# Attention with a gated projection on one core: two key blocks' value products in one run, ten slots for probabilities, four for x

## The reference

```
xn = layernorm(x)
q, k, v = xn @ Wq.T + bq, xn @ Wk.T + bk, xn @ Wv.T + bv        # 16 heads of 32
scores = q @ k.T / sqrt(32)
im = arange(1024) % 256
scores = where(im[:, None] >= im[None, :], scores, -1e30)
s = (softmax(scores) @ v) @ Wo.T + bo
w = (weights >= 0) * 2 - 1
g = silu(clip(xn @ w.T * scale + bias, -100, 100))
out = x + s * g
```

## Time and profile before

| | |
|---|---|
| median of 3 runs | 1834.33 us (1833.07 to 1834.93) |
| the profiled execution | 1834.76 us, of which the span from first to last instruction is 1832.9 us |
| mean granted PE clock | 0.994 |
| PE busy | 1761.5 us (96%), 12184 products |
| DVE busy | 1350.4 us (74%) |
| ACT busy | 977.1 us (53%) |
| POOL busy | 1225.6 us (67%) |

### The profile page before, as it was taken

The page is one execution under the profiler, slowest core; times in us unless marked ns, Lnnn a source line. Parts: engine busy times, 40 slices in busy tenths (PEclk is TensorE's granted clock), DMA queues, the critical chain, the costliest instruction groups (busy, mean ns, idle before and its releaser), DMA issues.

```text
span 1832.9 us, 34064 instructions
## 1 busy us (share of the span) xinstructions
PE 1761.5 (96%) x12184; PEld 796.1 (43%) x12184; DVE 1350.4 (74%) x2518; ACT 977.1 (53%) x1769; POOL 1225.6 (67%) x1066
## 2 busy tenths in 40 slices
PE   5989999999999999999999999999999999999888
PEld 3434444444444444444444444444444444444333
DVE  5878678776777877778777777778678786678652
ACT  4355665465545655456554565555655465554453
POOL 0066657775777567875587855786757775777782
PEclk9999999999999999999999999999999999999999
DMA  6311212221122211222122211222212221122111
GB/s 194 118 26 52 59 36 65 70 70 45 50 60 63 82 42 37 72 59 78 42 53 59 79 55 38 70 58 72 58 38 63 76 53 24 48 63 60 42 47 47
DMA packets 102137, 110.85 MB, mean 60 GB/s; under 512 B 24016, under 2 KB 76368, under 8 KB 101520
## 3 DMA queue, kind: packets, MB, share of 16 engines
q1 hardware_dynamic: 101008, 107.89, 21.4%
q10 hardware_dynamic: 960, 0.79, 0.2%
HBM read 41.23 MB, written 16.78 MB: 32 GB/s over the span
## 4 chain that ended last, share of the span: by engine, by line
PE 85%; DVE 5%; issue 3%; POOL 2%; ACT 2%; SPq 1%; DMA 1%; ACTq 0%; DVEq 0%; POOLq 0%
PE pJ L421 31%; PE pO L613 15%; PE pS L569 10%; PE pT L593 10%; PE pJ L502 3%; PE pT L553 3%; PE pJ L503 3%; PE pJ L506 3%; PE pS L572 3%; PE pT L589 3%; POOL acc L965 2%; DVE mx L873 1%; PE pS L433 1%; ACT PT L725 1%; SPq L1051 1%
## 5 line engine op out<-in xcount | busy, mean ns | idle before, releaser
L965 POOL TENSOR_TENSOR acc<-acc,PT 128x384 f32<-128x384 f32 (+1 forms) x744 | 871.1, 1197 | 402.2 <-PE pO L613 348.1
L873 DVE TENSOR_REDUCE mx<-pS 128x1 f32<-128x512 f32 (+3 forms) x1216 | 776.5, 652 | 273.1 <-PE pS L572 183.7
L725 ACT ACTIVATE PT<-pT 128x512 f32<-128x512 f32 (+1 forms) x960 | 538.1, 567 | 604.1 <-PE pT L593 536.8
L569 PE MATMUL pS<-QK 96*128 96x512 f16 (+3 forms) x1280 | 393.9, 318 | 20.9 <-DVE mx L873 18.1
L593 PE MATMUL pT<-QK 97*128 97x512 f16 (+3 forms) x1280 | 391.6, 317 | 2.6 <-ACT PT L725 1.3
L613 PE MATMUL pO<-PT,V 128*32 128x512 f32 (+3 forms) x2560 | 259.8, 478 | 8.4 <-ACT PT L725 8.2
L569 PEld LDWEIGHTS pS<-QK 96*128 96x128 f16 x1280 | 123.3, 97 | 246.1 <-DVE mx L873 82.5
L725 ACT ACTIVATE acc<-pT 128x512 f32<-128x512 f32 x256 | 151.1, 599 | 138.1 <-PE pT L593 138.0
L589 PE MATMUL pT<-QK 128*128 128x128 f16 x1024 | 179.9, 219 | 3.2 <-ACT PT L725 1.4
L572 PE MATMUL pS<-QK 128*128 128x128 f16 x1024 | 180.8, 220 | 0.6 <-DVE mx L873 0.6
L905 DVE TENSOR_TENSOR acc<-acc,PT 128x512 f32<-128x512 f32 x186 | 145.6, 783 | 16.4 <-POOL acc L965 16.4
(11 more groups left out here) (132 smaller groups left out, 2571.8 us busy)
## 6 DMA issues: line engine op xcount, KB each, us to landing
QK<-sg SPq DMA_DIRECT2D x756, 64.0 KB
xs<-in_x SPq DMA_DIRECT2D x62, 256.0 KB, 3.0
xr<-in_x SPq DMA_DIRECT2D x58, 256.0 KB, 3.0
out<-xr SPq DMA_DIRECT2D x56, 256.0 KB, 2.6
QK<-aT SPq DMA_DIRECT2D x256, 1.0 KB, 1.7
QK<-in_x SPq DMA_DIRECT2D x8, 256.0 KB, 4.1
out<-xs SPq DMA_DIRECT2D x6, 256.0 KB, 2.4
QK<-in_mqk SPq DMA_DIRECT2D x2, 512.0 KB, 9.6
```

The lines of the kernel that those rows point to most:

```text
L569: ins = e.matmul(s_bank("s", i)[:, base:base + wide], q4[0:96, j, qc], k4[0:96, j, 0:wide], start=True, stop=True)
L725: e.activation(to, t_bank("t", i)[:, 0:cols], ACT.Exp, scale=SS).then_inc(s_p, 1)
L873: e.tensor_reduce(mx[:, par, part, :].rearrange("p (j q) -> p j q", q=4)[:, heads[0]:heads[-1] + 1, qi], s_bank("s", i)[:, 0:cols].rearran ...
L965: e.tensor_tensor(a, a, PT[:, RING_AT[i] % NPT, 0:width * len(heads)].rearrange("p (j q) -> p j q", j=len(heads)), ALU.add).then_inc(s_ap, 1)
```

## The change

Value products of an even key block get the due time of the odd block after it (`kb | 1`), with 0.01 slot between the two; the row sums come 0.01 behind block 1 of the next unit instead of block 0. The ring of probabilities has ten slots, x four; the tiles 4 to 7 of batch 0 lie in `xr` and `On`, later tiles in slot i mod 4. In the last batch the gates 4 and 5 lie in `xr`, which adds a wait for the stores of earlier results; ACT's first two copies of pO into `On` wait for the first eight transposes. The due times of transposes, projections, splits, layer norm, gates, additions and evacuations are given new numbers, many of them one per tile.

```diff
-NPT = 8
+NPT = 10
-NXS = 6
+NXS = 4
...
 def at_s(i):
-    return SL * (m // 2 - 1) + (11 if m % 2 else 0) + i - S_FIRST[m] + 0.16
+    return SL * (m // 2 - 1) + (11 if m % 2 else 0) + i - S_FIRST[m] + 1.01
...
 def at_pv(n, kb):
-    return at_t(T_LAST[n, kb]) + 1.3
+
+    return at_t(T_LAST[n, kb | 1]) + 1.3 + 0.01 * (kb & 1)
...
-    return (at_pv(n + 1, 0) if n not in SUMMED else at_pv(n, 4 * (n % NQS) + 3)) + 0.01
+    return (at_pv(n + 1, 1) if n not in SUMMED else at_pv(n, 4 * (n % NQS) + 3)) + 0.01
...
     if kind == "x":
-        return 4 * SL * a + (-82.58 + 1.71 * b if b < 4 else -66.0 + 2.4 * (b - 4))
+        return 4 * SL * a + (-82.58, -80.5, -79.16, -77.98, -65.94, -63.09, -61.16, -60.29)[b]
...
     if kind == "f" and a == B - 1:
-        return 4 * SL * B + -92.42 + 9.0 * b
+        return 4 * SL * B + (-93.07, -76.47, -74.48, -63.0, -54.38, -48.26, -33.23, -23.9)[b]
...
     if kind == "o":
-        return wish("f", a, b) + 6.58
+        return 4 * SL * (a + 1) + (-10.95, -1.54, 8.03, 21.62, 34.05, 36.08, 39.44, 55.99)[b]
...
-LEN = {"x": 0.6, "sm": 0.63, "qk": 3.48, "v": 3.2, "f": 2.3, "o": 3.21, "b": 3.0}
+LEN = {"x": 0.24, "sm": 0.83, "qk": 3.52, "v": 3.34, "f": 2.46, "o": 3.28, "b": 3.0}
...
     if h == 0:
-        first = x0 + (-65.47 if b == 1 else -100.09)
-        return first, first + 4.71, 0.5, first + 16.92
-    return x0 + -12.63, x0 + -10.45, 0.3, x0 + -2.5
+        first = x0 + (-69.26 if b == 1 else -95.26)
+        return first, first + 4.82, 1.05, first + 17.99
+    return x0 + -11.82, x0 + -8.48, 0.42, x0 + -1.44
...
         def x_tile(i):
-            return xs[:, i, :] if i < NXS else xr[i - NXS][:, :] if i < NT else xs[:, (i - NT + NXS) % NXS, :]
+            return xr[i - 4][:, :] if i in (4, 5) else On[i - 6][:, :] if i in (6, 7) else xs[:, i % NXS, :]
...
         def gate(i):
-            return xs[:, i - NTILE + NT, :] if NTILE - NT <= i < NTILE - NT + NXS else U[i % 2][:, :]
+            k = i - NTILE + NT
+            return xs[:, k, :] if 0 <= k < 4 else xr[k - 4][:, :] if k in (4, 5) else U[i % 2][:, :]
...
             def take_outputs():
                 for n in range(NU):
-                    yield at_pv(n, 4 * (n % NQS) + 3) + 0.47
+                    yield at_pv(n, 4 * (n % NQS) + 3) + 0.71
+                    if n < 2:
+                        ln.wait_ge(s_xt, NT)
...
                         ln.wait_ge(s_f, i - NT + 1)
+                        if i - NTILE + NT in (4, 5):
+                            ln.wait_ge(s_o[i % 2], 16 * (NTILE - NT) // 2)
...
             def layer_norm():
-                        yield at_ln(hb)[0] + 0.59 * t
+                        yield at_ln(hb)[0] + 0.82 * t
...
@@ VectorE, additions
-                    yield at_t(i) + 1.9
+                    yield at_t(i) + 6.67
...
@@ GpSimd, additions
-                    yield at_t(i) + 1.7
+                    yield at_t(i) + 1.88
...
@@ GpSimd, normalise
-                    yield past("sm", n) + 2.02
+                    yield past("sm", n) + 1.42
-                    yield past("sm", n) + (3.77 if n in SUMMED else 6.04)
+                    yield past("sm", n) + (2.52 if n in SUMMED else 4.54)
```

More of the change, by code:

```diff
@@ L108, in at_pv @@
 def at_pv(n, kb):
-    return at_t(T_LAST[n, kb]) + 1.3
+    return at_t(T_LAST[n, kb | 1]) + 1.3 + 0.01 * (kb & 1)
 def at_sums(n):
-    return (at_pv(n + 1, 0) if n not in SUMMED else at_pv(n, 4 * (n % NQS) + 3)) + 0.01
+    return (at_pv(n + 1, 1) if n not in SUMMED else at_pv(n, 4 * (n % NQS) + 3)) + 0.01
 def wish(kind, a, b):
     if kind == "x" and a == 0:
-        return -83.44 + 1.0 * b if b < 4 else -74.12 + 0.86 * (b - 4)
+        return -85.75 + 1.01 * b if b < 4 else -75.64 + 1.49 * (b - 4)
     if kind == "x":
-        return 4 * SL * a + (-82.58 + 1.71 * b if b < 4 else -66.0 + 2.4 * (b - 4))
+        return 4 * SL * a + (-82.58, -80.5, -79.16, -77.98, -65.94, -63.09, -61.16, -60.29)[b]
     if kind == "qk" and a == 0:
-        return (-79.33, -74.04, -68.67, -68.11)[b]
+        return (-82.11, -74.55, -68.74, -67.05)[b]
     if kind == "qk":
-        return SL * (a - 2) + (6.01, 13.81, 20.23, 26.85)[b]
+        return SL * (a - 2) + (4.93, 12.99, 18.09, 22.56)[b]
     if kind == "v" and a == 0:
-        return -65.0 + 4.32 * b if b < 2 else -34.0 + 8.0 * (b - 2)
+        return -57.82 + 4.2 * b if b < 2 else -29.6 + 8.79 * (b - 2)
     if kind == "v":
-        return 4 * SL * a + -75.54 + 8.02 * b
+        return 4 * SL * a + (-75.54, -66.37, -61.36, -47.36, -45.38, -34.87, -27.37, -19.4)[b]
     if kind == "f" and a == B - 1:
-        return 4 * SL * B + -92.42 + 9.0 * b
+        return 4 * SL * B + (-93.07, -76.47, -74.48, -63.0, -54.38, -48.26, -33.23, -23.9)[b]
     if kind == "f":
-        return 4 * SL * (a + 1) + -18.0 + 9.5 * b
+        return 4 * SL * (a + 1) + (-16.72, -8.74, 1.03, 10.47, 19.69, 24.79, 39.0, 48.5)[b]
     if kind == "o" and a == B - 1:
-        return 4 * SL * B + (-20.72 + 3.58 * b if b < 4 else -4.1 + 2.56 * (b - 4))
+        return 4 * SL * B + (-21.43 + 4.39 * b if b < 4 else -4.06 + 3.75 * (b - 4))
     if kind == "o":
-        return wish("f", a, b) + 6.58
-    return 4.5
-LEN = {"x": 0.6, "sm": 0.63, "qk": 3.48, "v": 3.2, "f": 2.3, "o": 3.21, "b": 3.0}
+        return 4 * SL * (a + 1) + (-10.95, -1.54, 8.03, 21.62, 34.05, 36.08, 39.44, 55.99)[b]
+    return 3.86
+LEN = {"x": 0.24, "sm": 0.83, "qk": 3.52, "v": 3.34, "f": 2.46, "o": 3.28, "b": 3.0}
 PJ, PJ_ORDER, PJ_INDEX = {}, [], {}
@@ L190, in at_gate @@
     first = past("f", *divmod(i, NT)) + 0.5
-    return first + (0, 0.52, 2, 4.64, 5.5)[k] / 5.5 * min(5.5, past_o(i) + 0.3 - first)
+    return first + (0, -0.73, 2, 4.82, 5.5)[k] / 5.5 * min(4.98, past_o(i) + 0.3 - first)
 def at_ln(hb):
@@ L200, in at_ln @@
     if b == 0:
-        return x0 + -12.0, x0 + -6.4, 0.15, x0 + -4.86
+        return x0 + -17.86, x0 + -6.66, 0.21, x0 + -4.91
     if h == 0:
-        first = x0 + (-65.47 if b == 1 else -100.09)
-        return first, first + 4.71, 0.5, first + 16.92
-    return x0 + -12.63, x0 + -10.45, 0.3, x0 + -2.5
+        first = x0 + (-69.26 if b == 1 else -95.26)
+        return first, first + 4.82, 1.05, first + 17.99
+    return x0 + -11.82, x0 + -8.48, 0.42, x0 + -1.44
 def in_time(*strands):
@@ L334, in at_split @@
             key, i = w_pieces[n]
-            return (-79.38 + 0.3 * n if n < 2 else -71.84 + 0.4 * n if n < 6 else -65.59 + 0.3 * n if n < 8 else -40 + n if n < 12 else 10 + 0.5 * n)
+            return (-82.52 + 0.3 * n if n < 2 else -70.29 + 0.4 * n if n < 6 else -57.15 + 0.3 * n if n < 8 else -40 + n if n < 12 else 10 + 0.5 * n)
         def placed(gn, half):
@@ L654, in take_xt @@
                     for t in range(NT):
-                        yield past("x", b, t) + -0.06
+                        yield past("x", b, t) + -0.03
                         i = b * NT + t
@@ L666, in stage_qk @@
                     for o in range(4):
-                        yield past("qk", gn, o) + 0.09
+                        yield past("qk", gn, o) + -0.06
                         which, half = o % 2, o // 2
@@ L679, in place_first @@
                 for half in range(2):
-                    yield past("qk", 0, 2 * half + 1) + 1.99
+                    yield past("qk", 0, 2 * half + 1) + 2.45
                     cs = slice(512 * half, 512 * half + 512)
@@ L692, in store_v @@
                     for t in range(NT):
-                        yield past("v", b, t) + 0.35
+                        yield past("v", b, t) + 0.04
                         ln.wait_ge(s_vp, b * NT + t + 1)
@@ L738, in high_outputs @@
                     s, cs = gn % NSLOT, slice(qs * 512, qs * 512 + 512)
-                    yield past("sm", n) + (3.0 if n in SUMMED else 3.75)
+                    yield past("sm", n) + (3.48 if n in SUMMED else 3.59)
                     if gn >= NSLOT:
@@ L848, in take_xt @@
                     for t in range(NT):
-                        yield past("x", b, t) + 0.67
+                        yield past("x", b, t) + 0.36
                         i, ts = b * NT + t, slice(t * P, (t + 1) * P)
@@ L857, in stage_qk @@
                     for o in range(4):
-                        yield past("qk", gn, o) + 0.67
+                        yield past("qk", gn, o) + 0.8
                         which, half = o % 2, o // 2
@@ L867, in maxima @@
                 for i, (m, qi, part, width, heads) in enumerate(S_TILES):
-                    yield at_s(i) + 0.8
+                    yield at_s(i) + 0.49
                     par = m % 2
@@ L879, in shifts @@
                 for m in range(NU):
-                    yield at_s(S_FIRST[m + 1] - 1) + 0.52 + 0.8
+                    yield at_s(S_FIRST[m + 1] - 1) + 1.31 + 0.49
                     par = m % 2
@@ L909, in normalise @@
                 for n in range(NU):
-                    yield past("sm", n) + -0.16
+                    yield past("sm", n) + -0.11
                     ln.wait_ge(s_on, n)
```

(6 more changed lines are left out.)

## The result

The changed kernel takes 1786.71 us (median of 4 runs, 1782.61 to 1792.07) against 1834.48 before: a ratio of 0.9743, 95% interval 0.9713 to 0.9772. The forecast was 1795.6 with a range from 1784 to 1812. The profiled execution took 1782.61 us, span 1780.5 us, 52.2 us less than the profiled one before.

A forecast was written before the change was run, and what follows sets the result against it. PE, busy 1761.5 of 1832.9 us, was taken as the bound, so only its own instruction time could shrink: 1834.76 - 45.1 + 3.3 + 3 = 1796.0, less 0.4 for the profiled execution gives 1795.6 us; range 1784 to 1812.

The forecast's parts named there:

- Pairs: Values' products on PE: 192 pairs each save one exit and one entry of 0.235 us, 45.1 us in all.
- The choice at the hand-over into pO (0.88 us): Two groups writing pO: bounds 0.88 us (saving 0.235) and 1.00 us (saving 0); 0.235 was taken.
- Rivals C and D: C: only the entry gap goes, 1820.9, chance 0.04. D: something sorted between the two of a pair, 1834, chance 0.01.
- What can't be banked: Stretches where PE waits for others: some 14 pairs' saving only lengthens waits, 3.3 us given back (0 to 3.3).
- VectorE between runs: Middle: VectorE only just keeps pace between runs; PE's wait for maxima doubles, +6, less 1 and 2: +3 us.
- Rival A: VectorE falls behind in the long stretches, 0.02 us in each of 1036 slots: 1816, chance 0.13.
- GpSimd's additions and the ring: GpSimd's additions wait about four slots longer, 5.8 us, but it gets through and the ring of ten suffices: 0.
- rival B: Ring of probabilities: GpSimd's work piles up before late first adds and the exponential waits; slower, 1844, chance 0.05.
- Row sums later and x in four slots: Later sums still free acc in time, 0; x loads make VectorE wait 0.5 to 1 us in 7 batches, taken 0.
- Rival E: Head and tail come out better by 9 and 12 us of idleness: 1784, chance 0.09.
- All other retiming moves order only, taken 0: Projections, head and tail: retiming moves order only, between -10 and +10 us; taken 0.
- the cover: VectorE's additions move from +1.9 to +6.67, following GpSimd's delay; without this ScalarE would stop on the ring, and PE too.

The follow-up runs named there:

- e7: Changed kernel with the row sums of 62 units due 0.49 slot after the pair instead of 0.01, so in runs of their own: 1808.67 us, ratio 0.9858.
- e1: Changed kernel with each pair's odd block due 0.5 slot after the even one instead of 0.01, a score tile between: 1831.76 us, ratio 0.9983.
- e12: The changed kernel again, unaltered, timed beside the others: 1785.73 us, ratio 0.9734.
- e8: Changed kernel with ScalarE's four scalings of a batch's first half (batch 1 on) due 1.6 slots apart instead of 0.8: 1783.04 us, ratio 0.9730.
- e3: Changed kernel with the ring of probabilities at 8 instead of 10, x keeping four slots: 1784.72 us.
- e6: Changed kernel with the storage of before (ring of eight, six x slots, no added waits), all new due times kept: 1785.72 us.
- e4: Changed kernel with the first batch's old due times for transposes of x, projections, weight splits and layer norm: 1794.18 us, ratio 0.9782.
- e2: Kernel before with the pairs alone (new due times of values' products and row sums), every other time and the storage old: 1952.05 us, ratio 1.0645.

## Why the prediction was right, and where it was off

*Pairs, 45.1 us.* Right in mechanism and size: the medians give 0.232 us a pair, 44.5 us for 192, and e7 shows the edge for another bank. That e1 gives back 45.1 to the decimal is luck in part. Its 188 more runs are 44.2 us; its middle is 39.3 us longer where the pairs are worth 33.8, since its late row sums bring waits (7.0 us at L595), and its tail only 2.1 where they are worth 5.6. The choice at the hand-over into pO (0.88 us) was the right end of its bounds. The Trainium skill's drain ("TensorEngine Tiling (Array Packing)", Key Properties, with the 128 cycles of "TensorE: Matmul & The Clock Gate", Step-by-step: what each phase is for) would have given some 20 us: that changing the mode costs something agrees with the traces, the estimate from the drain's length alone covers less than half. Rivals C and D are out.

*What can't be banked, 3.3 us.* By the table, e1 against the kernel after is 6.1 us in the head and 2.1 in the tail, where the pairs are worth 5.6 each. So 3.5 us were lost, all of them in the tail; against the second execution (e12) it is 1.5 in the head and 3.2 in the tail. The size was about right, though part of the tail's loss may be clock (0.99 from 1650 to 1775 us in e1, 0.97 in the kernel after).

*VectorE between runs, +3.* The middle gave back 4.9 us, but not there: PE waited 0.9 us for maxima, not some 12, and 11.1 us at L591 for exponentials. Rival A did not come. The engine that fell behind was ScalarE. Its timeline in the kernel after (start, us, line), then PE's in the same time:

```profile
907.85 0.58 ACT L727 ACTIVATE PT<-pT 128x512 f32<-128x512 f32 x1
908.33 1.51 ACT L650 ACTIVATE xs<-xs,ab 128x512 f32<-128x512 f32 x2
909.74 0.48 ACT L727 ACTIVATE PT<-pT 128x384 f32<-128x384 f32 x1
```
```profile
908.49 0.23 PE L591 MATMUL pT<-QK 128*128 128x128 f16 x1 [0.24 <-ACT PT L727]
...
910.27 0.23 PE L591 MATMUL pT<-QK 128*128 128x128 f16 x1 [0.57 <-ACT PT L727]
```

Two scalings of layer norm stand before an exponential, and PE waits for the bank that it frees. Of the 34 waits at L591, 12 with 4.8 of the 11.1 us stand behind such scalings; the others stand mostly behind ScalarE's copies of x (L662) and of q and k (L676). What they replaced were the waits of the earlier trace rows, 8.9 us at the transposes of x and 6.0 for maxima. Named waits end before a product is due and so count too little: summing in the middle the distances from start to start over the shortest usual one of the same two kinds (excesses from 0.04 us on), PE loses 29.4 us after and 24.2 before, with 15.3 at L591 where there was nothing, and 4.4 at the transposes of x where there were 10.9. That sum accounts for the 4.9. I had counted rates (VectorE's 1.09 us a slot) and not looked at clusters on ScalarE. e8 took 4 us of the wait away, but no time that could be measured, so that ScalarE's clusters cost this time is read from the trace and not shown by a run.

*GpSimd's additions and the ring, 0.* Right: GpSimd now waits for pO at both units of a head group (53 times, 27 before; 254.0 us, 234.2 before), without cost. One sign of rival B did appear, ScalarE's wait for additions at 52.4 us (40.0 before in the same stretch), but in e3 it is 16.3 and PE's wait at L591 stays at 9.9, so it is not what PE waits for. Rival B had its margins right and its consequence wrong: e3 took two slots of ring away and nothing happened, since a stop of ScalarE costs only when PE is at the same bank.

*Row sums later and x in four slots, 0.* Right: VectorE waits 0.75 us for a load in six batches (forecast 0.5 to 1), and e6 finds no difference.

*Rival E, head and tail come out better, 1784.* It had a chance of 0.09 and came half true: the head gained 7.0 to 9.0 us beyond the pairs, the tail 3.3. The median is 2.7 us from it and 8.9 from the forecast.

*"All other retiming moves order only, taken 0".* This is the step that failed, in two ways. The new order of the head was worth 3 to 5 us (e4's trace). By the table, what came beside the pairs was -9.0 in the head, +4.9 in the middle and -3.3 in the tail, together -7.4 us, where I had +3.3 and +3: that is the distance from the sum's 1796.0 to the profiled 1782.6. (That execution was the fastest of the four, and their median lies 4 us above it, so the forecast's own distance is 8.9. By the estimates above up to 5.9 us of the gain at the two ends are clock, a term that the sum did not have.) And the pairs need the retiming: alone they cost 118 us (e2). I named VectorE's additions as the cover, and they are 70 us of the 165 between e2 and the changed kernel. The order of projections, transposes, layer norm and splits, which I priced at nothing, is 68.

## What to carry to other kernels

Where PE is full, look at the distance from start to start at the borders between kinds of products: a cost that no wait names is found there, and moving groups of a kind together gains the borders. A longer run on an in-order engine is also a longer gap for all that comes behind it: what another queue expects from before the run must be due before it, or its whole queue waits. Price the cover of such a change separately; here it decided between -48 and +118 us. A small shift of one due time can also put one more piece of work before another (here a sixth addition), and a test that shifts more than it means to test carries that along.

## What the runs showed of the hardware

Entering and leaving a run of 128x32 f32 products cost 0.093 + 0.139 us, independent of the width (128 to 512 columns) and of the bank written, and two groups that accumulate in one bank follow each other as closely as two in different banks (1.86 us for two of 512 columns). The changed kernel's runs spread over 9.5 us (1782.6 to 1792.1) where those of the kernel before spread over 2 (over 4 in the 13 beside e1). Their mean granted clocks were 0.997, 0.994, 0.996 and 0.998 for 1782.61, 1792.07, 1788.95 and 1784.47 us, so the two longer ones have the lower clock; no run here says why.
